# Value products in two groups a head, folding tiles ahead of them, modulation parts out of the first rows, keys by halves

## The reference, cut to what matters

```python
mod = (silu(c) @ wmod).reshape(4, 6, 1, -1)            # parts 0..5: sa, ca, ga, sb, cb, gb
ga, gb = floor_of_magnitude(ga), floor_of_magnitude(gb)  # at least 0.25, sign kept
h = layernorm(x) * (1 + ca) + sa
q = h @ q_w.T + q_b        # 16 heads of 32
k, v = h @ k_w.T + k_b, h @ v_w.T + v_b                # one head of 32, shared by the 16
attn = softmax(causal(q @ k.T / 32 ** 0.5))
x = x + ga * ((attn @ v) @ o_w.T + o_b)
h = layernorm(x) * (1 + cb) + sb
h = fwht(h * SU_ug) / 64
y = silu(h @ W_gate.T * s_gate) * (h @ W_up.T * s_up)  # 2048 wide
x = x + gb * (fwht(y * SU_dp) / 64 @ W_down.T * s_down)
```

## Time and profile before

| | |
|---|---|
| median of 3 runs (lowest, highest) | 2102.76 us (2100.27, 2103.38) |
| the profiled execution's own time | 2102.49 us |
| its span | 2100.8 us |
| TensorE busy | 2003.2 us (95%) |
| VectorE, ScalarE, GpSimd busy | 1200.7, 796.0, 165.9 us |
| value products L1470, 1920 matmuls | 302.0 us |
| score and maxima products L1447, L1300 | 258.6 and 248.1 us |
| granted TensorE clock, 0 to 19, 19 to 65, 65 to 998.68 us, then | 1.00, 0.89, 0.98, 1.00 of 2.4 GHz |

### The profile page before, as it was taken

The page is one execution under the profiler, slowest core; times in us unless marked ns, Lnnn a source line. Parts: engine busy times, 40 slices in busy tenths (PEclk is TensorE's granted clock), DMA queues, the critical chain, the costliest instruction groups (busy, mean ns, idle before and its releaser), DMA issues.

```text
span 2100.8 us, 27156 instructions
## 1 busy us (share of the span) xinstructions
PE 2003.2 (95%) x9504; PEld 1497.5 (71%) x9504; DVE 1200.7 (57%) x2611; ACT 796.0 (38%) x1334; POOL 165.9 (8%) x522
## 2 busy tenths in 40 slices
PE   7998999999999889888999999999999999999998
PEld 3565666656666556555788888888888888888887
DVE  5677675776677556666544554455454555445434
ACT  3356552655456444456222222322322222223111
POOL 0111111111112111112000000000000000000000
PEclk9999999999999999999999999999999999999999
DMA  6442334224432465752634434334344343343441
GB/s 189 141 108 67 89 101 128 69 59 121 115 97 69 134 206 184 240 185 55 221 130 149 173 123 168 121 124 171 126 140 149 129 164 122 129 171 120 145 136 61
DMA packets 113662, 279.87 MB, mean 133 GB/s; under 512 B 27754, under 2 KB 33130, under 8 KB 113400
## 3 DMA queue, kind: packets, MB, share of 16 engines
q1 hardware_dynamic: 104168, 248.71, 38.2%
q10 hardware_dynamic: 9360, 29.43, 3.9%
HBM read 199.15 MB, written 35.93 MB: 112 GB/s over the span
## 4 chain that ended last, share of the span: by engine, by line
PE 51%; DVE 1%; DMA 1%; SPq 0%; ACT 0%; issue 0%; POOL 0%; POOLq 0%; DVEq 0%; ACTq 0%
PE banks L1246 33%; PE banks L1402 16%; PE banks L1344 1%; PE banks L1338 1%; DMA upgate_raw<-in_w_ug 0%; PE banks L1470 0%; DVE out_sb L1040 0%; DMA inverse_sums_dram<-sums 0%; PE banks L1447 0%; DVE out_sb L1031 0%; ACT probs L770 0%; DMA o_group<-o_raw 0%; PE banks L1313 0%; DVE masked_scores L864 0%; SPq L421 0%
## 5 line engine op out<-in xcount | busy, mean ns | idle before, releaser
L1246 PE MATMUL banks<-h_t_split,w_ring 128*128 128x512 f32 x3072 | 717.4, 389 | 1.4 <-DVE w_ring L1005 1.3
L1246 PEld LDWEIGHTS banks<-h_t_split,w_ring 128*128 128x128 f32 x3072 | 576.6, 188 | 121.7 <-DVE w_ring L1005 2.2
L709 ACT ACTIVATE silu_gate<-banks,scale_upgate 128x512 f32<-128x512 f32 x128 | 88.3, 690 | 801.8 <-PE banks L1246 801.8
L770 ACT ACTIVATE probs<-banks 128x512 f32<-128x512 f32 x576 | 318.0, 595 | 169.3 <-PE banks L1447 148.3
L1402 PE MATMUL banks<-d_ring,y_split 128*128 128x512 f32 x1536 | 370.7, 390 | 0.1
L1013 DVE SCALAR_TENSOR_TENSOR y<-banks,scale_upgate,silu_gate 128x512 f32<-128x512 f32 x128 | 95.9, 749 | 432.4 <-ACT silu_gate L709 432.4
L1402 PEld LDWEIGHTS banks<-d_ring,y_split 128*128 128x128 f32 x1536 | 287.3, 188 | 59.5 <-DVE y_split L1019 0.5
L1470 PE MATMUL banks<-probs,v_ones 128*64 128x128 f32 (+3 forms) x1920 | 302.0, 445 | 1.2 <-POOL probs L843 1.2
L1300 PE MATMUL banks<-k_stack,q_stacks 96*128 96x512 f32 (+3 forms) x768 | 248.1, 366 | 34.6 <-DVE fold_split L957 16.8
L1447 PE MATMUL banks<-q_stacks,k_stack 98*128 98x512 f32 (+3 forms) x768 | 258.6, 380 | 0.0
L1470 PEld LDWEIGHTS banks<-probs,v_ones 128*64 128x64 f32 x1920 | 148.4, 140 | 154.6 <-issue 125.9
(11 more groups left out here) (122 smaller groups left out, 1258.2 us busy)
## 6 DMA issues: line engine op xcount, KB each, us to landing
upgate_raw<-in_w_ug SPq DMA_DIRECT2D x128, 512.0 KB, 4.2
d_ring<-down_split_dram SPq DMA_DIRECT2D x128, 512.0 KB, 3.2
q_stacks<-q_split SPq DMA_DIRECT2D x192, 128.0 KB, 2.4
o_group<-o_raw SPq DMA_DIRECT2D x128, 128.0 KB, 2.3
x<-in_x SPq DMA_DIRECT2D x32, 256.0 KB, 3.3
o_group<-inverse_sums_dram SPq DMA_DIRECT2D x64, 128.0 KB, 2.7
x_and_residual<-in_x SPq DMA_DIRECT2D x32, 256.0 KB, 3.4
x_dram<-x_and_residual SPq DMA_DIRECT2D x32, 256.0 KB, 2.6
```

What stands on the lines that cost most here:

```text
L770: nc.scalar.activation(pr[:, u, :], score_bank[:, at % SLOTS_SCORE, :], ACT.Exp, scale=SCALE).then_inc(exped, 1)
L1246: ins = nc.tensor.matmul(out, weights(a, k), moving(m, k), start=(k == 0 and a + m == 0), stop=(last and k == kts - 1 and a == 1))
```

## The change

Value products come in two groups a head, behind unit 4 (second part of the head before) and unit 8 (first part), with five and four units ahead of them; they have 1280 and 1024 columns of each half, in 7 and 5 products where it was 5, 5 and 5. The evacuations move to units 8 and 4, ahead of the tiles of `units[u]` on ScalarE. Tiles of `ends` go ahead of the group on TensorE and ScalarE, and the folding tiles stand at units 4 and 8, in four heads also at 2 and 6. At the start, part 2 goes from the first rows to behind the keys, part 5 beside the maxima of head 0, part 3 behind their transposition, part 4 into units 0 to 3 of head 0; the weight splits and the load of the exponential's table go between row tiles. VectorE stacks the keys by halves, and `kst_ready` counts two for each batch entry. The crossings move from head 61 to 62.

The diff, without the edits of three waits that only count anew:

```diff
...
 NU = len(UNITS)
-THIRD = 3
+PART_ENDS, PARTS_OF_HEAD = (4, 8), 2
...
 WEIGHED = [
-    (0, [(0, 0, 0, 0, 512, 0), (1, 1, 1, 128, 384, 0), (0, 2, 2, 384, 128, 128), (1, 2, 2, 256, 128, 0), (1, 1, 3, 384, 128, 384)]),
-    (1, [(0, 3, 0, 512, 512, 0), (1, 4, 1, 512, 512, 0), (0, 5, 2, 512, 384, 0), (1, 2, 6, 768, 256, 256), (1, 5, 2, 896, 128, 384)]),
-    (1, [(0, 7, 4, 512, 512, 0), (1, 6, 3, 512, 512, 0), (0, 8, 5, 640, 256, 0), (1, 8, 5, 896, 128, 256), (1, 8, 7, 896, 128, 384)]),
+    [(0, 0, 0, 0, 512, 0), (1, 4, 1, 512, 512, 0), (0, 3, 0, 512, 512, 0), (1, 1, 1, 128, 384, 0), (1, 1, 3, 384, 128, 384),
+     (0, 2, 6, 768, 256, 256), (1, 2, 2, 256, 256, 0)],
+    [(0, 5, 2, 512, 512, 0), (1, 6, 3, 512, 512, 0), (0, 7, 4, 512, 512, 0), (1, 8, 5, 640, 384, 0), (1, 8, 7, 896, 128, 384)],
...
 PART_BANK = {0: 0, 1: 1, 2: 2, 5: 0, 3: 6, 4: 7}
-BESIDE_ROWS = {("rows", 0, 0, k): (2, k) for k in range(KT)}
-BESIDE_MAXIMA = {("max", 0, 2 * k + 1): (3, k) for k in range(KT)}
+BESIDE_MAXIMA = {("max", 0, 2 * k + 1): (5, k) for k in range(KT)}
+PART_BEHIND = {("kv", 0, 1): 2, ("top", 0): 3}
...
-FOLDS = [("across", left, u) for left in (19, 18, 17, 16, 15) for u in (2, 5, 8)] + [("across", 14, 2)]
-FOLDS += [("along", left, u) for left in (12, 11, 10, 9, 8) for u in (2, 5, 8)] + [("along", 7, 2)]
-BLOCK_IN, STAT_LEFT, NORM_LEFT, CROSS_LEFT, CAST_LEFT = 7, 6, 5, 3, 1
-TURNS, HADS = [(4, 2), (4, 5), (4, 8), (3, 2)], [(2, 2), (2, 5), (2, 8), (1, 2)]
+FOLDS = [("across", left, u) for left, us in ((19, (4, 8)), (18, (4, 8)), (17, (2, 4, 6, 8)), (16, (4, 8)), (15, (4, 8)), (14, (2, 4, 6, 8))) for u in us]
+FOLDS += [("along", left, u) for left, us in ((12, (2, 4, 6, 8)), (11, (2, 4, 6, 8)), (10, (4, 8)), (9, (4, 8)), (8, (4, 8)), (7, (4, 8))) for u in us]
+BLOCK_IN, STAT_LEFT, NORM_LEFT, CROSS_LEFT, CAST_LEFT = 7, 6, 5, 2, 1
+TURNS, HADS = [(4, 4), (4, 8), (3, 4), (3, 8)], [(2, 8), (1, 2), (1, 4), (1, 6)]
...
                     load_upgate(0)
-                if left == CROSS_LEFT:
+                if left == AHEAD + 1:
...
             def evacuate(H, c):
-                act.wait_ge(pv_done, H * THIRD + (3 if c else 1))
+                act.wait_ge(pv_done, H * PARTS_OF_HEAD + c + 1)
...
                     if H:
-                        act.wait_ge(pv_done, (H - 1) * THIRD + (2 if u == 2 else u // THIRD + 1))
+                        act.wait_ge(pv_done, (H - 1) * PARTS_OF_HEAD + (1 if u <= PART_ENDS[0] else 2))
                     nc.scalar.activation(pr[:, u, :], score_bank[:, at % SLOTS_SCORE, :], ACT.Exp, scale=SCALE).then_inc(exped, 1)
-                    if u == THIRD - 1 and H:
+                    if (H, u) == (0, KT):
+                        copy_part(4)
+                    side_step(ends[u])
+                    if u == PART_ENDS[0] and H:
                         evacuate(H - 1, 1)
-                    if u == 2 * THIRD - 1:
+                    if u == PART_ENDS[1]:
...
                     side_step(units[u])
-                    side_step(ends[u])
...
                         deviations(0)
-                    if left == CROSS_LEFT and u == NU - 1:
+                    if left == CROSS_LEFT and u == 4:
...
             layer_norm_deviations(nc, act, T, eps, 0)
-            nc.scalar.activation(m1[:, 0:1], eps[:], ACT.Exp)
...
                 layer_norm_rows(nc, act, T, 0, t, "first_last_xn")
-            act.wait_ge(kvw_in, 64)
-            nc.scalar.activation(kvw[:, 0], kv_raw, ACT.Copy).then_inc(kvw_hi, 1)
-            act.wait_ge(qw_raw_in, 16)
-            nc.scalar.activation(qw[:, 0], q_raw[:, :, 0:P], ACT.Copy).then_inc(q0_hi, 1)
             act.wait_ge(mod_ready, 1)
-            before = side_before()
-            for key in before:
+            for key in side_before():
+                if key == ("top", 0):
+                    copy_part(5)
                 side_step([key])
-                if key == ("kv", 0, 0):
+                if key == ("rows", 0, 0, 1):
+                    act.wait_ge(qw_raw_in, 16)
+                    nc.scalar.activation(qw[:, 0], q_raw[:, :, 0:P], ACT.Copy).then_inc(q0_hi, 1)
+                if key == ("rows", 0, 0, 3):
+                    act.wait_ge(kvw_in, 64)
+                    nc.scalar.activation(kvw[:, 0], kv_raw, ACT.Copy).then_inc(kvw_hi, 1)
+                    nc.scalar.activation(m1[:, 0:1], eps[:], ACT.Exp)
+                if key == ("kv", 0, 1):
                     copy_part(2)
-                if key == ("kv", 0, 1):
-                    copy_part(5)
-            for m in (3, 4):
-                copy_part(m)
+            copy_part(3)
...
-            def stack_keys(b):
...
-                for h in range(2):
-                    side_taken(dve, ("kv", b, h))
-                chain.link(nc.vector.tensor_copy(kst[0:96, b % 2, :], kv[0:96, :]))
-                nc.vector.tensor_tensor(kst[32:64, b % 2, :], kv[32:64, :], kst[32:64, b % 2, :].bitcast(F32), ALU.subtract).then_inc(kst_ready, 1)
+            def stack_keys(b, h):
+                at = slice(h * HALF, (h + 1) * HALF)
+                side_taken(dve, ("kv", b, h))
+                chain.link(nc.vector.tensor_copy(kst[0:96, b % 2, at], kv[0:96, at]))
+                nc.vector.tensor_tensor(kst[32:64, b % 2, at], kv[32:64, at], kst[32:64, b % 2, at].bitcast(F32), ALU.subtract).then_inc(kst_ready, 1)
...
                         split_rows(key)
-                    elif key[0] == "kv" and key[2] == 1:
-                        stack_keys(key[1])
+                    elif key[0] == "kv":
+                        stack_keys(key[1], key[2])
...
                         block_rows(0, u - 4)
-                    if left == CROSS_LEFT and u in (4, 6):
-                        cross(0, u // 2 - 2)
-                    if left == CROSS_LEFT - 1 and u in (0, 1):
-                        crossed_rest(0, (2 * u, 2 * u + 1))
+                    if left == CROSS_LEFT and u in (1, 3):
+                        cross(0, u // 2)
+                    if left == CROSS_LEFT and u in (5, 6):
+                        crossed_rest(0, (2 * u - 10, 2 * u - 9))
...
                                             ALU.subtract, ALU.mult).then_inc(T["first_xn"], 1)
-                dve.wait_ge(kvw_hi, 1)
-                nc.vector.tensor_tensor(kvw[:, 1], kv_raw, kvw[:, 0].bitcast(F32), ALU.subtract).then_inc(kvw_ready, 1)
-                dve.wait_ge(q0_hi, 1)
-                nc.vector.tensor_tensor(qw[:, 1], q_raw[:, :, 0:P], qw[:, 0].bitcast(F32), ALU.subtract).then_inc(q0_ready, 1)
...
                 side_step([key])
+                if key == ("rows", 0, 0, 2):
+                    dve.wait_ge(q0_hi, 1)
+                    nc.vector.tensor_tensor(qw[:, 1], q_raw[:, :, 0:P], qw[:, 0].bitcast(F32), ALU.subtract).then_inc(q0_ready, 1)
                 if key == ("q", 0, 0):
+                    dve.wait_ge(kvw_hi, 1)
+                    nc.vector.tensor_tensor(kvw[:, 1], kv_raw, kvw[:, 0].bitcast(F32), ALU.subtract).then_inc(kvw_ready, 1)
+                if key == ("rows", 0, 1, KT - 1):
...
                     if H % HEADS == 0:
-                        pe.wait_ge(kst_ready, b + 1)
+                        pe.wait_ge(kst_ready, 2 * (b + 1))
...
-            def weigh(H, third):
...
-                c, parts = WEIGHED[third]
+            def weigh(H, part):
...
                 b = H // HEADS
-                if third == 0:
+                if part == 0:
                     pe.wait_ge(masked, H * len(TRIANGLES) + 3)
+                    pe.wait_ge(exped, H * NU + PART_ENDS[0] + 1)
...
                         side_taken(pe, ("v", b))
-                elif third == 1:
-                    pe.wait_ge(exped, H * NU + 2 * THIRD)
+                    for c in range(2):
+                        if H:
+                            pe.wait_ge(o_copied[c], H)
+                        else:
+                            pe.wait_ge(part_copied, PARTS.index(3) + c + 1)
...
                     pe.wait_ge(masked, (H + 1) * len(TRIANGLES))
-                if third < 2 and H:
-                    pe.wait_ge(o_copied[c], H)
-                elif third < 2:
-                    pe.wait_ge(part_copied, PARTS.index(3) + c + 1)
-                begun = {0, 1} if third == 2 else set()
-                for i, (half, u, kt, q0, w, col) in enumerate(parts):
-                    ends = third != 1 and half not in [p[0] for p in parts[i + 1:]]
+                begun = {(half, 1) for half in range(2)} if part else set()
+                for i, (half, u, kt, q0, w, col) in enumerate(WEIGHED[part]):
+                    c = q0 // HALF
+                    ends = c == part and (half, c) not in [(p[0], p[3] // HALF) for p in WEIGHED[part][i + 1:]]
                     last = nc.tensor.matmul(obank[half * 2 * HD:(half + 1) * 2 * HD, c, q0 - c * HALF:q0 - c * HALF + w],
-                                            vs[:, b % 2, kt, :], pr[:, u, col:col + w], start=half not in begun, stop=ends)
-                    begun.add(half)
```

(23 more changed lines are left out.)

6 lines of the change are left out of this document (3 added, 3 removed).

## The result

The changed kernel takes 2130.19 us (median of 4 runs, 2127.79 to 2132.46), the kernel before 2101.76 us (4 runs, 2100.27 to 2103.38): the ratio is 1.0135 with a 95% interval of 1.0117 to 1.0153, so it is slower by 28 us, where 18 us faster was forecast.

A forecast was written before the change was run, and what follows sets the result against it. TensorE, busy 860.03 of attention's 933.68 us, was taken as the bound. Terms 16 + 15 + 5.5 + 2.5 - 8 - 13 sum to an 18 us gain: 2102.49 - 18 = 2084.5 us, forecast 2076 to 2093 (0.60).

The forecast's parts named there:

- what gets later: Attention: second half evacuated at unit 4, not 2, delaying SyncE's gather and residual loads; 8 us lost (3 to 16).
- tiles at unit 4: Row and key heads: ScalarE takes unit 4's tile only after value group and evacuation; 13 us lost (4 to 20).
- Five units in a row use three side banks and three score banks: Quiet heads: VectorE's reductions (3.9 us) end inside five units and their group, so the whole 0.37 us a head stays.
- The late residual: Heads 19, 35 and 51: third output tile's residual loads behind the gather, issued 4.8 us later; 1 us lost each.
- VectorE or the ring binds: Rival, attention: five units without a pause wait for side banks; 2 us gain remains, 2100.5 us; chance 0.08.
- Value groups: Attention: one group fewer a head saves 0.37 us, counted for 44 heads; 16 us gained (9 to 20).
- Folding tiles: Folding heads: 24 of 32 tiles stand ahead of a group that covers their rounding; 15 us gained (10 to 20).
- Start: Before attention: VectorE's row splits start earlier, second query product at 33.1, not 38.71; 5.5 us gained (1 to 8).
- cold start: Rival: first query product slow after idling, start gains 2.5 instead of 5.5, head 0's group costs 1; 2088.5 us; chance 0.10.
- The rival on the slower side: Attention: query products don't hide VectorE's gather wait at unit 6, 14 heads lose 4 us each; 2140.5 us; chance 0.05.
- Keys by halves: Key stacking on VectorE: the split burst is covered by part 2's products at the start; costed at nothing.
- Last heads: Heads 60 to 63: crossings move a head later, where no maxima are; 2.5 us gained (-3 to 6).

The follow-up runs named there:

- turning SyncE's order: Changed kernel with SyncE storing unit 1's output tile and loading the residual behind it before it gathers the head before; 2121.22 us, ratio 1.0085 to the kernel before.
- the mixed kernel: Kernel with the changed kernel's start and three value groups, but two groups in 22 heads; 2072.32 us, ratio 0.9850 to the kernel before.

## Why the prediction was wrong

**What failed** is the pricing of the longer run of units, in two terms. In *what gets later*, the nine output heads had 4 us, less 3.3 for their groups; they lost 16.8. In *tiles at unit 4* the mechanism was right and the size was not: 13 us forecast, 25.1 measured. These two explain 28 of the 46 us between forecast and result; the other 18 are small: 6.5 in the folding heads, 3.9 in heads 6, 8, 22 and 38, 3.2 in head 0, 3.5 behind head 57, 1.1 in the start.

The term *tiles at unit 4* was mis-sized. Turning ScalarE's order alone gives back 22.0 of its 25.1 us, so the predicted wait behind the evacuation is nearly all of it. Of the 12 us that it was short, some 8.5 are the lower clock (below), which the term left out. The wait of 1.4 us of the tile itself, which it left out too, stays when the order is turned, with +2.5 and +0.6 us.

The output heads failed by a step: "Five units in a row use three side banks and three score banks", and "the reductions (3.9 us) end inside them". That was worked out for a quiet head and holds there. A side tile in the second unit of the run gives VectorE two operations more, the maxima queue behind them, and the tile at unit 4 waits 1.3 to 2.0 us for its bank; with three groups one stood between them, and the wait in head 21 was 0.36 us. Moving the output tiles off units 1, 4 and 7 took 19 us out of these nine heads, at most 5 of them lower clock, with nothing else changed. That the group gave VectorE the time is read from the order of its work in head 21 and not tested by itself. The late residual, for which the forecast had 1 us at each of three places, came too: turning SyncE's order is worth 3.3 us in head 20 (its granted clock also goes from 0.94 to 1.00), 1.7 in head 36 and 0.3 in head 52. The longer wait at its place, 2.94 us against 1.10, was for the store, which the forecast didn't name. The rival *VectorE or the ring binds* named such waits for quiet heads, where they did not happen.

**The clock was left out of these terms.** In heads 26 and 27 TensorE has the same work, and the same waits within 0.01 us, and they differ by 1.7 us at 1.00 and 0.90. Three of the six row heads (10, 27 and 43) took 16.2 to 16.3 us in this way, and the same three did in the traces of all five kernels that leave the two groups, these tiles and ScalarE's order as they are. An estimate of the whole: a head's length times what its granted clock lacks to 1.00 (16.30 x 0.105 = 1.7 us in head 27), summed over the 64 heads, is 18.8 us before and 39.3 after. So of the 32.2 us that the 64 heads lost at most 20.5 are lower clock, and the rest is what the waits took by themselves, less what the groups and the tiles' order gained. By heads it is 5.1 us more in the row heads, 3.4 in the key heads, 3.4 in the output heads and 5.1 in heads 6, 8, 22 and 38, whose whole +3.9 it can be. The traced execution is no exception: the mean clock was 0.977 to 0.980 in all four of the changed kernel, and 0.984 to 0.990 in those of the kernel before that ran beside the experiments. The prediction priced a slow stretch only for its rivals.

**Value groups: right.** 0.37 us a head forecast, 0.38 measured over the 25 heads (0.57 in heads 15, 23, 31 and 39, which have neither queries nor waits).

**Folding tiles: right mechanism, wrong in company.** Alone the move gives 17 us, within 10 to 20. In the changed kernel the folding heads gain 10.2 us, groups included, where 16.7 were forecast, since four heads hold four tiles: there the tile at 4 or 8 waits 0.94 and 0.83 us itself. The prediction left these eight their old 0.65 us each and said "less where a bank is still busy at unit 8"; that case came.

**Start: right, and its cover not.** In the changed kernel:

```profile
26.38 4.53 PE L1249 MATMUL banks<-h_t_split,qw_group 128*128 128x512 f32 x12 [2.07 <-ACT kv L610]
...
34.34 4.56 PE L1249 MATMUL banks<-h_t_split,qw_group 128*128 128x512 f32 x12 [2.94 <-DVE h_t_split L896]
...
60.59 0.50 PE L1450 MATMUL banks<-q_stacks,k_stack 98*128 98x512 f32 x1
```

The second query product stands at 34.34 (33.1 forecast), the first score at 60.59 (59.5). In the traces of all 14 kernels with the new start the first score stands at 57.9 to 61.8, 59.2 in the mean, and in the four with the old one at 64.8 to 66.6, 65.8 in the mean: 6.6 us gained, 5.5 forecast. Both query products ran slow here, as in the rival *cold start*; in the mixed kernel's profiled execution (22 heads with two groups) both ran fast:

```profile
26.97 2.97 PE L1263 MATMUL banks<-h_t_split,qw_group 128*128 128x512 f32 x12 [2.08 <-ACT kv L624]
...
33.36 3.00 PE L1263 MATMUL banks<-h_t_split,qw_group 128*128 128x512 f32 x12 [2.98 <-DVE h_t_split L910]
```

Its first score is at 58.06. The two executions idle alike ahead of these products. In the changed kernel the granted clock was 1.00 up to 26.4 us, 0.78 from there to 34.3 and 0.70 from there to 40; in the mixed kernel it was 0.85 from 15 to 26.4 us and 1.00 from there to 40. The Trainium skill (TensorE: Matmul & The Clock Gate, "What's actually happening") has a throttle as the default that activity releases, and the prediction took from it that these products come slow: the trace agrees in one execution and not in the other. Part 4 is covered in head 0 with three groups (21.58 us against 21.37 before) and not with two (24.59 us). That "without the cover it costs 3.5 more" is so near the 3.2 measured is luck: TensorE is busy 21.16 and 23.58 us in that head, and the 3 us between the two are about what the lower clock can take (1.00 with three groups, 0.86 with two, 0.84 before).

**The rival on the slower side** gave 2140.5, near the result, for a reason that did not act. In head 32 VectorE waits 2.75 us for the gather (2.65 worked out), and the query products start half a microsecond earlier than that wait ends and run at full speed:

```profile
537.32 0.19 DVE L908 TENSOR_TENSOR sums<-sums 128x32 f32<-128x32 f32 x1 [2.75 <-DMA o_group<-o_raw]
```

```profile
536.82 5.74 PE L1249 MATMUL banks<-h_t_split,qw_group 128*128 128x512 f32 x24
```

Heads 16, 24, 32 and 40 are 0.3 to 0.4 us faster than before. The tiles at unit 4 alone came past the bound of their term (20 us) with their 25.1, and no rival took the forecast's own two losses, larger and together, as a case.

**Keys by halves** were costed at nothing and are worth 5.7 us in the trace when alone. In the changed kernel that gain is lost in the same three heads' +7.6. The trace of before shows TensorE's wait of 0.82 us for a maximum ahead of the values in head 28; it was not read.

**Last heads.** 2.5 us forecast, less 2 for head 60; 1.2 lost, and 1.8 more in head 63. The new places of the crossings and tiles bring the loss in head 63: with three groups they cost it 1.7 us too, and gain 3.0 in heads 58 to 62. In head 62, TensorE and then ScalarE:

```profile
1009.75 0.51 PE L1450 MATMUL banks<-q_stacks,k_stack 98*128 98x384 f32 x2 [2.52 <-ACT probs L770]
...
1010.81 3.90 PE L1473 MATMUL banks<-probs,v_ones 128*64 128x512 f32 x14
```

```profile
1007.02 2.19 ACT L692 ACTIVATE h_crossed_split<-h_t 128x512 fp32r<-128x512 f32 x4
1009.12 2.04 ACT L770 ACTIVATE probs<-banks 128x512 f32<-128x512 f32 x4
```

The exponentials stand behind four roundings of the crossings, as worked out, and the group that follows the wait is slow.

**Open** is why one head of two alike keeps its clock. That is also the most of what heads 22 and 38 lose, 1.4 and 1.7 us: their long wait is as before (1.96 and 1.95 us for 2.03 and 2.02), one of 0.44 us is new, and the granted clock is 0.77 where it was 0.87.

## What to carry to other kernels

Merging pauses on the busiest engine saves their fixed cost, but the pauses were also where the engines beside it caught up. Before a run is lengthened, follow the slowest neighbour through the run with every side tile in it, in the fullest heads and not in the quiet one, and place the tiles behind the first unit of the run. Price each new wait of TensorE of about a microsecond with and without a stretch at lower clock behind it: here that was up to 20 of the 32 us that the heads lost. Try each part of a bundled change alone: here the folding tiles' order (-17 us) and the keys by halves (-10 us by the ratio, -5.7 in the trace) were gains that a merged change hid. The parts don't add: what goes with the groups was worth 7 us beside two of them and 28 beside three.

## What the runs showed of the hardware

The granted clock fell after waits of 0.8 to 3 us, and not always. In the kernel before, heads 12, 28 and 44 have the same waits of TensorE within 0.01 us, the longest 0.81 and 0.82 us, and take 23.27 us at a granted clock of 1.00 and 24.82 and 24.90 at 0.93. With the keys by halves, and so without the wait, head 28 took 22.42 us at 1.00: the 0.82 us cost 2.4, some 1.6 of them by the clock.

The same instructions met different clocks in two executions. The kernel with three groups and the new start and the one with the new crossings are the same up to head 60. Head 38 took 14.61 us at a granted clock of 0.77 in the first and 11.97 at 1.00 in the second, and head 8 20.41 at 0.92 and 23.26 at 0.78. So a head can differ by up to 3 us without any change to it, and a single trace cannot show a gain under some 3 us in the sum.
